# Side work of an attention kernel dealt out by round: one turn in a light round, seven in a heavy one, and the next turn's beginning put ahead of the first visit

## The reference, cut to what matters

```python
logits = (x @ Wr)...; node_probs = softmax(logits)             # 16 heads, 4 nodes each
expected_pos = cumsum(node_probs, axis=2) - node_probs
pos = clip(expected_pos, 0, 2047); pf = pos.astype(int32); frac = pos - pf
cos = cos_c[pf] + frac * (cos_c[pc] - cos_c[pf])               # and sin
cos_w = einsum('bhsk,bhskd->bhsd', node_probs, cos)            # and sin_w
q_r = q * cos_w + rotate_half(q) * sin_w                       # and k_r
scores = q_r @ k_r^T * SCALE + log(node_probs @ node_probs^T + 1e-8), causal
out = softmax(scores) @ v; x = x + out @ Wo
```

## Time and profile before

| | |
|---|---|
| median of 3 runs | 2907.16 us (2905.93 to 2914.46) |
| the profiled execution | 2896.46 us, its span 2894.6 us |
| mean granted TensorE clock | 0.925 |
| attention's lead | about 347 to 536 us |
| units, rounds 0 to 7 | about 536 to 2531 us |
| feed-forward ahead and behind | the rest |

### The profile page before, as it was taken

One profiled execution on the slowest core, in us unless ns is written; L12 is line 12 of the kernel. 1 busy time (PEld: TensorE's weight loads), 2 busy tenths in 40 slices (PEclk: granted clock), 3 DMA queues, 4 the chain that ended last, 5 costly groups with the idle time before them and its releaser, 6 DMA issues. The chain is left out here.

```text
span 2894.6 us, 104325 instructions
## 1 busy us (share of the span) xinstructions
PE 2448.1 (85%) x45990; PEld 1896.7 (66%) x45990; DVE 1711.7 (59%) x3627; ACT 1702.9 (59%) x2174; POOL 997.9 (34%) x1497
## 2 busy tenths in 40 slices
PE   7298444587899999899999989999999999973885
PEld 4165222466788887778888777888877888841553
DVE  7732278788576567866566786666676111167431
ACT  6222123456677777667777766777776777662221
POOL 1188700334222224423222442222244222110787
PEclk9699776799999999999999999999999999986997
DMA  6555401221212112212111221211122111162565
GB/s 233 160 103 101 78 18 30 60 53 47 60 57 56 48 46 79 66 49 59 55 53 52 79 66 53 58 53 53 54 74 69 44 47 49 42 204 72 105 102 74
DMA packets 185109, 207.28 MB, mean 72 GB/s; under 512 B 35984, under 2 KB 151712, under 8 KB 184480
## 3 DMA queue, kind: packets, MB, share of 16 engines
q1 hardware_dynamic: 158880, 165.60, 19.3%
q0 software_dynamic: 24576, 34.10, 7.6%
q10 hardware_dynamic: 1152, 0.26, 0.0%
HBM read 131.68 MB, written 76.02 MB: 72 GB/s over the span
## 5 line engine op out<-in xcount | busy, mean ns | idle before, releaser
L1697 PEld LDWEIGHTS at_mix<-at_val,at_ew 128*64 128x64 f32 x34816 | 1223.7, 138 | 241.3 <-issue 36.0
L1281 ACT ACTIVATE at_ew<-at_ring 128x1024 f32<-128x1024 f32 (+1 forms) x1280 | 1124.7, 898 | 364.4 <-PE at_ring L1679 358.2
L1697 PE MATMUL at_mix<-at_val,at_ew 128*64 128x68 f32 x34816 | 1263.0, 224 | 44.7 <-DVE at_mixed L1543 28.7
L1679 PE MATMUL at_ring<-at_qT,at_kT 98*64 98x512 bf16 (+3 forms) x5120 | 698.9, 353 | 57.9 <-ACT at_ew L1281 35.8
L1202 POOL TENSOR_SCALAR_AFFINE_SELECT at_ew<-at_ew 128x256 f32<-128x256 f32 x512 | 294.3, 579 | 1074.2 <-ACT at_ew L1281 1073.5
L1543 DVE TENSOR_TENSOR at_mixed<-at_mix,at_prob 128x272 f32<-128x272 f32 x256 | 112.3, 439 | 440.4 <-PE at_mix L1697 439.1
L1679 PEld LDWEIGHTS at_ring<-at_qT,at_kT 98*64 98x64 bf16 x5120 | 228.5, 112 | 111.4 <-ACT at_ew L1281 47.6
L1224 POOL TENSOR_TENSOR at_val<-at_vo,at_val 128x256 f32<-128x256 f32 x384 | 267.4, 717 | 7.5
L344 POOL DMA_INDIRECT out_dram<-ffn_xn,ffn_idx_all x128 | 210.0, 1641 | 43.4 <-issue 35.0
L334 POOL DMA_INDIRECT ffn_xn<-table,ffn_idx_all x128 | 126.2, 986 | 278.4 <-DMA ffn_idx_all<-ffn_idx_hi 240.3
L1762 PE MATMUL at_side<-at_w_all,at_turned 128*64 128x512 f32 (+1 forms) x1024 | 197.8, 531 | 13.8 <-DVE at_bounded L1536 5.2
(11 more groups left out here) (243 smaller groups left out, 2727.1 us busy)
## 6 DMA issues: line engine op xcount, KB each, us to landing
table<-ffn_xn SPq DMA_DIRECT2D x32, 512.0 KB, 6.3
q_parts<-at_parts SPq DMA_DIRECT2D x64, 192.0 KB, 2.5
k_parts<-at_parts SPq DMA_DIRECT2D x64, 192.0 KB, 3.0
at_qT<-q_parts SPq DMA_DIRECT2D x128, 96.0 KB
at_kT<-k_parts SPq DMA_DIRECT2D x64, 192.0 KB
ffn_front<-in_L_attn_x_dram SPq DMA_DIRECT2D x16, 512.0 KB, 5.3
ffn_w_in<-in_L_ffn_w_dram SPq DMA_DIRECT2D x32, 256.0 KB, 3.6
at_xin<-out_dram SPq DMA_DIRECT2D x32, 256.0 KB, 6.0
```

The lines of the kernel that those rows point to most:

```text
L1281: act.activation(ew[u % NE_BUF][:, a:b], ring[u % 2][:, a:b], ACT.Exp).then_inc(s["exp_ready"], 1)
L1679: lastm = pe.matmul(ring[u % 2][h:h + HALF, at:at + (CH - t) * P], kT[q][:, kc + j * P + h:kc + j * P + h + HALF], qT[q][:, qc + t * P:qc ...
L1697: m = pe.matmul(mix[block_of[u] % 2][h:h + HALF, t * K * VW:(t + 1) * K * VW], ew[u % NE_BUF][:, col + h:col + h + HALF], val[q][:, tile0 ...
```

## The change

Turns are laid out by round. Round 0 keeps four turns of 24 units. Every heavy round has seven turns of 32 units (kind MID), every light round after round 0 one turn of 96 units (kind WIDE). There are 35 turns where there were 34, each with its own tables. The bursts, in which TensorE weighs unit u in unit u, now last six units, from 22 in MID and from 69 in WIDE. A `head_start` does the first steps of turn 0 (pair 5) before the first visit. VectorE's steps are cut finer and its lead is reordered: the two halves of the rotation stand around `shift_logits`, the statistics and the joining of the halves ahead of `positions`, the bound behind the node products. In MID and WIDE turns the node products and sums are four instructions of half the size each. `turn_rotated` issues eight 128-column transposes where it issued sixteen 64-column matmuls with the identity.

```diff
-    turns, at = [], 0
-    while at < U:
-        m = len(turns)
-        turns.append((at, SHORT if m < N_SHORT else LONG))
-        at += turns[-1][1]
+    rounds = [first_unit[v] for v in range(V) if v == 0 or visits[v][1] != visits[v - 1][1]] + [U]
+    turns = []
+    for r in range(len(rounds) - 1):
+        size = rounds[r + 1] - rounds[r]
+        count, kind = (N_SHORT, SHORT) if r == 0 else (N_MID, MID) if r % 2 else (1, WIDE)
+        turns += [(rounds[r] + n * (size // count), size // count, kind) for n in range(count)]
...
+    STORE_AT = (20, 22, 53)
...
-        BURST = 26
+        BURST = (None, 22, 69)
...
             for t in range(LEAD):
                 lead(t, t - 1 if t else None)
+            head_start(LEAD, LEAD - 1)
             first_visit()
...
-                    if at == 0:
+                    if at == 0 and new != LEAD:
                         load_x(new)
...
-                    if at == (10 if short else 14) and new is not None:
+                    if at == (10, 12, 28)[kind] and new is not None:
                         add_up(new)
...
-                SHORT_AT = (3, 6, None, 8, 9, 12, 15, 18, 16, 23, 20)
-                LONG_AT = (4, 6, 10, 8, 16, 18, 20, 23, BURST + 2, BURST + 4, BURST + 3)
+                SHORT_AT = (3, 6, None, 8, 9, 12, 15, 19, 17, 23, 16)
+                MID_AT = (4, 6, 9, 8, 14, 16, 18, 21, 24, 28, 22)
+                WIDE_AT = (6, 12, 18, 17, 36, 38, 44, 52, 71, 68, 55)
+                AHEAD = (0, 1, 3)
+
+                def head_start(new, fin):
+                    for n in AHEAD:
+                        steps(new, fin)[n]()
...
-                def lead(new, fin):
+                def head_start(new, fin):
                     if fin is not None:
                         turn_weights()
-                        rotate(fin)
+                        rotate(fin, 0)
                     shift_logits(new)
+                    if fin is not None:
+                        rotate(fin, 1)
                     node_softmax(new)
+                    statistics(new + 1)
+                    if fin is not None:
+                        join_halves()
                     positions(new)
-                    statistics(new + 1)
-                    angles(new)
+                    whole_positions()
+                    first_angles(new)
+                    count_turns()
+                    angles()
+                    absolute_angles(new)
+
+                def lead(new, fin):
+                    head_start(new, fin)
                     normalise(new + 1)
                     if fin is not None:
                         largest_squares(fin)
+                    for c in (0, 2):
+                        node_products(new, c, 2)
+                    if fin is not None:
                         bound(fin)
-                    node_products(new)
-                    node_sums(0)
-                    node_sums(2)
+                    for c in (0, 2):
+                        node_sums(c, 2)
...
+                AT = {"weights": (1, 1, 2), "rotate": (2, 2, 4), "rotate_2": (2, 3, 6), "join": (3, 4, 8), "squares": (14, 18, 44),
+                      "bound": (20, 23, 58), "residual": (None, 9, 22), "shift": (6, 5, 14), "softmax": (8, 8, 18),
+                      "positions": (10, 12, 28), "whole": (10, 12, 29), "first_angles": (11, 13, 31), "count_turns": (12, 14, 33),
+                      "angles": (13, 15, 36), "absolute": (13, 16, 38), "statistics": (15, 17, 41), "normalise": (23, 24, 60)}
+                PRODUCTS_AT = ({18: 0, 21: 2}, {26: 0, 28: 1, 29: 2, 31: 3}, {75: 0, 79: 1, 83: 2, 87: 3})
+                SUMS_AT = ({19: 0, 22: 2}, {27: 0, 29: 1, 30: 2, 31: 3}, {77: 0, 81: 1, 85: 2, 89: 3})
...
-                                    for h in range(0, P, HALF):
-                                        at = (g * 4 + n) * P + h
-                                        lastm = pe.matmul(side[h:h + HALF, n * GP + g * P:n * GP + (g + 1) * P],
-                                                          qkr[:, at:at + HALF], ident[:, :],
-                                                          start=(n % 2 == 0 and g == 0), stop=False, skip_group_check=True)
+                                    at = (g * 4 + n) * P
+                                    lastm = pe.matmul(side[:, n * GP + g * P:n * GP + (g + 1) * P], qkr[:, at:at + P], ident[:, :],
+                                                      is_transpose=True, start=(n % 2 == 0 and g == 0), stop=False, skip_group_check=True)
...
                 SHORT_AT = (1, 4, None, None, 9, 10, 13, 16, 19, 21)
-                LONG_AT = (1, 3, 7, 9, 13, 15, 17, 20, 24, BURST)
+                MID_AT = (1, 3, 6, 8, 11, 13, 15, 18, 22, 24)
+                WIDE_AT = (2, 8, 14, 20, 26, 34, 40, 48, 56, 64)
+                AHEAD = (0, 1, 4)
...
-                    if not short and (at == 0 or at >= BURST):
+                    if kind != SHORT and BURST[kind] <= at <= BURST[kind] + 5:
                         weigh_until(u)
```

More of the change, by code:

```diff
@@ L825, in build_attention @@
     LEAD = 5
-    SHORT, LONG = 24, 40
-    N_SHORT = 4
+    SHORT, MID, WIDE = 0, 1, 2
+    N_SHORT, N_MID = 4, 7
     TAIL = TP - 4
@@ L1054, in build_attention, with schedule @@
         PRIME_S, PRIME_U, PRIME_M, PRIME_E = 2, 2, 2, NE_BUF
[L1056 removed]
+        def schedule(lead, head_start, first_visit, unit, last_projections):
             for t in range(LEAD):
                 lead(t, t - 1 if t else None)
+            head_start(LEAD, LEAD - 1)
             first_visit()
[L1061 to L1063 removed]
+            for m, (start, size, kind) in enumerate(turns):
+                for at in range(size):
+                    unit(start + at, at, kind, new_of(m), fin_of(m), posts.get(m))
             last_projections()
@@ L1247, in first_visit, with unit @@
                     weigh_visit(1)
-                def unit(u, at, short, new, fin, post):
+                def unit(u, at, kind, new, fin, post):
                     if u in late_of:
@@ new lines, in unit @@
+                    per = 2 if kind == SHORT else 1
+                    if fin is not None:
+                        if "weights" in step:
+                            turn_weights()
+                        if "rotate" in step:
+                            rotate(fin, 0)
+                        if "rotate_2" in step:
+                            rotate(fin, 1)
+                        if "join" in step:
+                            join_halves()
+                        if "squares" in step:
+                            largest_squares(fin)
+                        if "bound" in step:
+                            bound(fin)
@@ new lines, in unit @@
+                    if post is not None and "residual" in step:
+                        add_residual(post, 0, 1)
+                    if new is not None:
+                        if "shift" in step:
+                            shift_logits(new)
+                        if "softmax" in step:
+                            node_softmax(new)
+                        if "positions" in step:
+                            positions(new)
+                        if "whole" in step:
+                            whole_positions()
+                        if "first_angles" in step:
+                            first_angles(new)
+                        if "count_turns" in step:
+                            count_turns()
+                        if "angles" in step:
+                            angles()
+                        if "absolute" in step:
+                            absolute_angles(new)
+                        if at in PRODUCTS_AT[kind]:
+                            node_products(new, PRODUCTS_AT[kind][at], per)
+                        if at in SUMS_AT[kind]:
+                            node_sums(SUMS_AT[kind][at], per)
```

106 lines of the change are left out of this document (46 added, 60 removed).

## The result

The changed kernel takes 2946.68 us (median of 4 runs, 2944.30 to 2950.74), the kernel before 2907.72 us (2905.93 to 2914.46) in the same comparison: a ratio of 1.0131 with a 95% interval of [1.0110, 1.0152]. It is 39 us or 1.3% slower; 17 us slower was predicted, 2924 us in a range of 2862 to 2958. The profiled execution took 2944.43 us, with a span of 2942.7 at a mean clock of 0.922.

What follows compares the result with a forecast made beforehand. TensorE was taken to bound heavy rounds, VectorE the lead, with late VectorE and ScalarE steps idling light rounds and round 0. Terms -85 + 35 + 59 + 27 - 12 - 7 = +17 on 2907 gave 2924 us, range 2862 to 2958.

Steps and rivals of the forecast that it cites:

- Side work out of the light rounds: Light rounds 2, 4 and 6: less side work and less idle shorten them, -85 us together (bounds -101 and -67).
- The same work in the heavy rounds: Heavy rounds 1, 3, 5, 7: seven turns for six and extra posts on a full TensorE, +35 us.
- Where the sines stand: MID turns: `project_qk` no longer covers ScalarE's sines, so TensorE waits 2.8 us in 21 turns, +59 us (48 to 69).
- The clock: Behind the sines' wait in MID turns: half clock loses 1.3 us per turn, +27 us (0 to 42).
- Round 0: First round: cheaper transposes, `take_middle_off` ahead of the sines' wait and the head start, less a longer load wait; -12 us.
- The lead: Before the first score: shorter waits for positions and root, against pair 5's early steps; -7 us (-12 to +2).
- (a): Rival, heavy rounds: the move works and the sines stay covered; -69 us, 2838 us; chance 0.15.
- (b): Rival: the sines' wait exists but the clock holds, and light rounds lose 10 us more idle; about 2887 us; chance 0.15.
- (c): Rival: light rounds keep most idle because VectorE's first WIDE steps have little slack; 20 us more, 2944 us; chance 0.14.
- (d): Rival, `turn_rotated`: transposes count as rest for the clock, costing 36 us in all; 2960 us; chance 0.03.
- (e): Rival, `turn_rotated`: transposes are four times faster, eight taking about 0.5 us; about 2905 us; chance 0.03.

Runs made afterwards that it cites:

- e9: e5 with the edits of e6 and e7 added: 2808.33 us, 0.9695 of the kernel before.
- e2: Changed kernel with the sines two units behind `project_qk` in MID and WIDE turns, first MID node products and sums one unit later: 2861.08 us, 0.9878 of the kernel before.
- e3: Kernel before with `project_qk` of long turns moved two units later, into the unit of the sines: 2952.67 us, 1.0194 of the kernel before.
- e6: e5 with `shift_logits` at unit 4 of MID turns, ahead of the second rotation (5) and the join (6): 2826.70 us, 0.9718 of the kernel before.
- e1: Changed kernel with `next_rsqrt` of the short turns set back from unit 16 to 20: 2915.56 us, 1.0054 of the kernel before.
- e8: e5 without `head_start`, turn 0 doing all of pair 5 after the first visit begins: 2857.95 us, 0.9827 of the kernel before.
- e7: e5 with ScalarE's `softmax_exp` ahead of `copy_qk` in the lead: 2848.38 us, 0.9795 of the kernel before.
- e5: Changed kernel with the edits of e1 and e2 together: 2854.55 us, 0.9819 of the kernel before.
- e4: Kernel before with only the eight 128-column transposes in `turn_rotated`: 2878.51 us, 0.9938 of the kernel before.

## Why the prediction came out as it did

**Direction right, size half.** +17 was predicted and the stages give +35 (the medians +39). The largest cause is the sines, as put, with 66 us of wait and clock. By stage the errors are +14.6 in round 0, +13.8 in the heavy rounds, +4.3 in the lead and -15 in the light rounds. With round 0 as predicted the total would have come out right within a few us, but partly by luck: the light rounds and the heavy ones were off by nearly the same and cancelled, and inside the heavy rounds +13 of work and 14 of a wait not foreseen stood against 20 too much for the sines and the clock. By its own steps:

**Side work out of the light rounds:** right, and larger, -100 for -85. The idle fell to 5.9, 6.2 and 4.6 us, 16.7 in all against 16 by my sum. So the error was in the busy time, and much of it in the base: I took the 137.8 us busy of the earlier trace rows as work at full clock, though the clock of that row is 0.97 and 10 us of the round were at the lower level. At half speed these hold up to 5 us that are no work, of the 6.6 by which round 2 was busy less (114.1) than my 120.7. After the change round 2 has no stretch at the lower level.

**The same work in the heavy rounds:** +35 was too little. e9 does the same steps with about 1 us idle in each heavy round, and its four rounds take 359.5, 365.4, 365.8 and 295.1 us: +48. In round 3 that is 15.6 for 11.5. Of the difference 1.4 is more of the values' product falling inside the round (6376 to 6431 recorded instructions of L1697 and its successor, 226.6 to 228.0 us), and 0.8 is idle (1.0 after 0.2). The lines of side work and posts grew by 12.1 us of busy time, overlaps between them counted twice, for my 11.5; the last 1 to 2 us I can't assign. Put per turn, e9 gives (365.4 - 295.1) / 7 = 10.0 us where I took 9.6.

**Where the sines stand:** the mechanism was right in place and releaser, and shown from both sides by e2 and e3. The 21 waits lie between 1.86 and 2.56 us, 48 us in all, for 59 predicted: the mean of 2.3 is my lower bound, so of the 1.0 us for a ScalarE that had not caught up nothing shows.

**The clock:** 11 of the 21 waits are followed by 3.4 us at the lower level, and there `project_qk` takes 4.8 to 5.3 us, 5.2 in the mean, for the 3.6 of the others. That is 11 x 1.6 = 18 us, for 27 predicted.

**Not in my sum:** the waits at units 8 and 9, 14 us in the changed kernel's heavy rounds. I listed VectorE's finer steps at no cost, covered by its being busy only 221 of 347 us. That cover is an average. The queue is in order, and what counts is when `shift_logits` comes, behind the weights, two rotations and the join, and behind what the turn before left over; e6 moved it one unit up and the second rotation and the join two down, for 28 us. That the order is enough to mend it e6 shows; how much of the wait comes from the sums at the end of the turn before no run separates. With these four terms the heavy rounds add up to 48 + 48 + 18 + 14 = 128 of +134.8. Waits at units 30 and 31 are 1.6 more, and the lower clock behind the unit-8 wait of 1437.03 up to 1.7; 3 to 4 us stay open.

**Round 0, the step that failed:** "Four turns save 0.7 each by the transposes, and 0.9 each since `take_middle_off` now stands ahead of the sines' wait". It looked at what stands at the sines alone. The same table moves `next_rsqrt` four units up, and I put that at nothing, without asking what it waits for. The runs show in its place a ScalarE that waits 17.6 us in three turns for VectorE's variance, and e1 gives its price, 17 us of round 0: +2.6 measured for -12 predicted. By itself that is as large as the whole difference between +17 and +35. The rest of the step came out: turn 0 gained the 8 that I counted for the head start, though by e8 the head start is 5.9 of them, and the load for round 1, for which I had added 1.5 us, cost nothing more.

**The lead:** -2.7 for -7. The waits for the positions went as put. What was late next, the softmax's exponential behind `copy_qk` on ScalarE, I had not asked for; e7 gives its 7.5 us back. My sum had the head start pay for itself and no more, in two terms, -8 in turn 0 and +9.6 ahead of the first score; e8 bears out the balance at smaller sizes, 5.9 and 5.2.

**The rivals.** (a), sines that stay covered, is out by 21 rows of waits; with the cover given back and the root mended, e5 takes 0.9819 of the old time, which is 2855. (b) is out in the main: its clock held in 10 of 21 turns only. The light rounds were 15 us shorter than by my sum, for its 10, though not by idle, of which they kept what I had taken. (c) is out by the windows of the light rounds. (d) and (e) are out by e4: -18 us, no fall of the clock at the transposes, and 1.09 us for eight, not 0.5.

## What to carry to other kernels

When a table moves steps in queues that are in order, walk through every entry that moved, not only the long one, and write down for each what it waits for and what stands behind it; VectorE was free 42% of the span and still late by 4.4 us where it counted. Look also at the end of a turn, since what is late there is late in the next. Where one engine does a long step that the other soon needs (here 4.7 us of ScalarE between two exponentials), ask what the other still has ahead of its wait, in the queue and not only at the same unit number: `project_qk` behind the wait covered nothing in e3 and in the changed kernel. And before a change is dropped because it came out slower, look for the few waits it created: here three table edits and one exchange turned +1.3% into -3.05%.

## What was not expected of the hardware

Waits of nearly the same length, 1.86 to 2.56 us, at the same place in the same turn, left the granted clock at full speed in 10 of 21 turns, and in the other 11 were followed by 3.4 us at the lower level. The rows don't show what decides. The price is set by what stands behind the wait: here it is TensorE's longest step, so a fall adds 1.6 us in the mean (5.2 for 3.6) to a wait of 2.3.
